# Layer 0's experts: ScalarE and VectorE take up the side work one block later, TensorE's program unchanged

## The chip, the cores and the metric

The kernel runs on one core of a Trainium2 chip. The metric is the device time of one execution in microseconds (us). Before the change it is 1907.77 us, the median of 3 runs (1901.92 to 1912.78). Engines are named as the profile does: PE is TensorE, DVE VectorE, ACT ScalarE, POOL GpSimd and SP the engine that issues the DMAs.

## The reference, cut to what matters

Two transformer layers act on x of 4 x 1024 tokens with 128 channels, each layer with 16-head attention and a mixture of experts with the best two of E gates. The stage in question begins behind the attention of layer 0:

```python
x = layernorm(x + attention0(x, Wqkv, Wout))          # causal
# experts of layer 0: E = 8, F = 256, K = 2
scores = x @ Wg.T
topk_scores, topk_idx = top_k(scores, 2)
gating = one_hot(topk_idx) weighted by softmax(topk_scores)
h = silu(x @ W1[e].T) * (x @ W2[e].T)                 # for every expert e
x = layernorm(x + sum_e gating[e] * (h @ W3[e].T))
# then layer 1: attention with rotary embedding, experts with E = 4
```

## The kernel before

Every engine has its own program, and the programs meet at semaphores only; each engine takes its instructions strictly in the written order. The stage "experts of layer 0" is `pe_end`, `act_end` and `dve_end` with `layer` 0. It treats the 4096 tokens in 8 chunks of 512 (`pe_chunk`, `act_chunk`, `dve_chunk`), and each chunk in 16 blocks n = 0 to 15, one for every 128 of the 8 x 256 hidden columns.

The main work of block n:

- TensorE, `pe_hidden` (L971): six matmuls (three partial products each for W1 and W2) put the two hidden sums into PSUM. It is issued one block ahead: in step n stands the hidden work of block n + 1 (`h_lead`).
- ScalarE: `act_s` = silu of the first sum (L1176).
- VectorE: `lin_u` = second sum times the gate row (L1375), then `hid` = `act_s` times `lin_u` (L1379).
- TensorE, `pe_product` (L1067): `hid` times W3 is summed up in `bank0`. It waits for `hid_ready`.

Beside the blocks run three other tasks, spread over the 16 steps by a table of numbers, `plan[0]`, in `pe_beside`, `act_beside` and `dve_beside`. For the chunk behind ("back"), the second layernorm and layer 1's q, k and v; for the chunk ahead ("front"), layer 0's output projection, layernorm and router. The plan gives: y_turn 1, norm2 3, x2_turn 4, q 5, k 6, v 7, o_turn 8, o_proj 9, norm 10, x_turn 11, router 12, weigh 13, g_turn 14. Most of these steps hand a result from TensorE to ScalarE or VectorE in one step, and TensorE uses their answer in the next step:

- x2_turn (4): TensorE transposes `x_out`, which VectorE normalised in step 3 (L1221). ScalarE copies it to `xt2` (L1122), which q (L1003) reads in step 5.
- q and k (5, 6): VectorE turns them by the rotary tables (`rot`, L1306 and L1307); TensorE's k and v wait for `rot_done`, since they write the same banks.
- v (7): VectorE copies `v_all` (L1312), subtracts `qk_lo` twice (L1316) and copies `os_` (L1321), for which o_turn (8) waits (`o_in`).
- o_turn (8): ScalarE copies `ot` (L1132), which o_proj (9) reads. VectorE adds and takes statistics (L1326, L1213, L1216), POOL takes the root, VectorE normalises `xs` (L1221) in step 10, and x_turn (11) waits for it.
- x_turn (11): ScalarE copies `xt` and `x_hi`, and the router (12) reads `xt`.
- router (12): VectorE finds the best two (L1229 to L1232). ScalarE's exp (L1145) and VectorE's gates (L1254 to L1275) stand in step 13, and g_turn (14) waits for them.
- g_turn (14): ScalarE copies `gate_t` (L1150), which gate row 0 of the next chunk (L980, step 15) reads.

A gate row is one matmul (L980) into the single bank `bank1`. ScalarE copies it to `gate_bc` (L1161), and the next gate row waits for that copy (`gbc_saved`). Row 0 of a chunk belongs to step 15 of the chunk before, and row e to step 2(e - 1).

How far ScalarE and VectorE are behind is set by `LATE`, one number for each layer. In step n, both do the main work of block n, and then the side work of step n - LATE. In TensorE's program `LATE` doesn't occur. At the start of chunk c the side work that is left over from chunk c - 1 comes first:

```python
m = n - LATE[layer]
if m >= 0:
    act_aside(act, st, c, m, back, front, 1 - par, layer)
elif not isinstance(c, int) or c > 0:
    act_aside(act, st, c - 1, m + SPC, None, c, par, layer)
```

Of the kernel before, what the change touches and what calls it, by code (L numbers as in the profile page):

```python
# [39 lines left out]
PAIRS_STEP = 2  # L40
SB = 3
HB = 4
LATE = (0, 2)
PAIR_HEADS = (2, 0, 3, 1)
ROWS = 2 * SLOT

# [159 lines left out]
def build_program(nc, d, out):  # L206
    with ExitStack() as ctx:
# [955 lines left out]
        def act_aside(act, st, c, n, back, front, par, layer):  # L1163

            per = SPC // n_exp[layer]
            act_beside(act, st, n, back, front, par, layer)
            e = n // per + (layer == 0)
            if n % per == per - 2 and e < n_exp[layer]:
                act_gate_rows(act, st, c, e, layer)

        def act_chunk(act, st, c, par, back, front, layer):
            for n in range(SPC):
                act.wait_ge(st.h_ready, c * SPC + n + 1)
                wait_used(act, st.hid_ready, c * SPC + n - 1)
                if layer == 0:
                    nc.scalar.activation(act_s[n % 2][:, :], hbank[n % 2], ACT.Silu).then_inc(st.s_done, 1)  # L1176
                else:
                    if n % 2 == 0:
                        wait_used(act, st.y_done, c * SPC + n - HB + 1)
                        nc.scalar.activation(hid_hi[n % HB][:, :], hbank[h_of[1][n]], ACT.Gelu, bias=be1[:, n:n + 1])  # L1180
                    nc.scalar.activation(act_s[n % 2][:, :], hbank[h_of[1][n]], ACT.Gelu,  # L1181
                                         bias=be1[:, n:n + 1]).then_inc(st.s_done, 1)
# [5 lines that stand above are left out]
            if layer == 0:  # L1188
                act.wait_ge(st.y_done, (c + 1) * SPC)
                nc.scalar.activation(y_sb[:, :], bank[0][:, :], ACT.Copy).then_inc(st.y_saved, 1)  # L1190

        def act_end(act, st, layer):
# [11 lines left out]
            act_chunk(act, st, 2 * B - 1, 1, 2 * B - 2, None, layer)  # L1204
            for n in range(SPC - LATE[layer], SPC):
                act_aside(act, st, 2 * B - 1, n, None, None, 0, layer)
# [144 lines left out]
        def dve_weigh(dve, st, c, e):  # L1351

            dve.wait_ge(st.gbc_saved, 1 + c * E1 + e + 1)
            dve.wait_ge(st.y_done, c * SPC + (e + 1) * (SPC // E1))
            if e == 0:
                wait_used(dve, st.y_turned, c)
            elif e > 1:
                dve.wait_ge(st.y_sum, 2 * c + e - 1)
            nc.vector.scalar_tensor_tensor((y_sb if e == 0 else y_tmp)[:, :], y_bank[e % 2], be2[:, e:e + 1],
                                           gate_bc[e % 2][:, :], ALU.add, ALU.mult).then_inc(st.y_used, 1)  # L1360
            if e > 0:
                dve.wait_ge(st.y_used, c * E1 + e + 1)
                nc.vector.tensor_tensor(y_sb[:, :], y_sb[:, :], y_tmp[:, :],
                                        ALU.add).then_inc(st.y_sum if e < E1 - 1 else st.y_saved, 1)

        def dve_chunk(dve, st, c, par, back, front, layer):
            per = SPC // n_exp[layer]
            for n in range(SPC):
# [12 lines left out]
                else:  # L1381
                    wait_used(dve, st.y_done, c * SPC + n - HB + 1)
                    dve.wait_ge(st.s_done, h_banks[layer] + c * SPC + n + 1)
                    if n % 2 == 1:
# [3 lines left out]
                                            ALU.subtract).then_inc(st.hid_ready, 1)  # L1388
                    if n % per == LATE[1] and (n > per or back is not None):
                        dve_weigh(dve, st, c if n > per else back, (e - 1) % E1)  # L1390
                m = n - LATE[layer]
                if m >= 0:
# [263 lines left out]
```

## Time and profile before

| | |
|---|---|
| median of 3 runs | 1907.77 us (1901.92 to 1912.78) |
| profiled execution, its own time | 1903.04 us |
| its span, first to last instruction | 1901.2 us |
| mean granted TensorE clock | 0.961 |
| busy, whole span | PE 90%, DVE 76%, ACT 63%, POOL 5% |
| experts of layer 0 | about 387 to 787 us |
| experts of layer 1 | about 1600 to 1880 us |

In the rows, a line such as "L1176 ACT ACTIVATE act_s<-hid_pair" is one instruction group with its line in the kernel, engine, operation, output and input. A timeline row has its start and its duration in front. A bracket at its end is the time for which the engine was idle before, and who ended this. Matmuls overlap in the rows: their starts show the pace, and the end of one is modelled. The share of busy time is an average over stages with different limits, so a change in one stage is read from that stage.

### The profile page before, as it was taken

What the parts mean: (1) busy time and instruction counts of PE and PEld (TensorE: products, weight loads), DVE (VectorE), ACT (ScalarE), POOL (GpSimd) and SP (SyncE); (2) the same over time, 40 slices, a digit from 0 to 9 for tenths busy, and PEclk for the clock granted to TensorE, in tenths of its full rate; (3) what the DMA queues carried; (4) which work ended last, traced back from release to release, by engine and by line L of the source; (5) the groups of instructions that cost most, each with busy time, mean ns of one, the idle gap of its engine ahead of it and who ended that gap; (6) DMA issues with size and microseconds to landing.
All of it is one profiled execution on the core that took longest, in us unless ns stands there. A gap on an engine that the chain in (4) does not pass through costs nothing.

```text
span 1901.2 us, 31713 instructions
## 1 busy us (share of the span) xinstructions
PE 1705.9 (90%) x9440; PEld 866.5 (46%) x9440; DVE 1451.9 (76%) x2661; ACT 1201.6 (63%) x1858; POOL 94.3 (5%) x123
## 2 busy tenths in 40 slices
PE   6899999799999999759999999999999986888887
PEld 3333433356565666423333333333333324656665
DVE  2788888757777777567898888889889825777776
ACT  3788888643444444206777777777777775665565
POOL 1000000001101110110000000000000000000010
PEclk9899999899999999958999999999999997998999
DMA  7431212101110011120010000000000001000000
GB/s 223 128 106 50 61 49 61 67 1 34 34 34 17 18 33 33 34 74 2 27 39 21 21 22 21 21 21 21 21 22 21 21 1 45 7 7 6 6 11 12
DMA packets 44967, 69.07 MB, mean 36 GB/s; under 512 B 16080, under 2 KB 25168, under 8 KB 44256
## 3 DMA queue, kind: packets, MB, share of 16 engines
q1 hardware_dynamic: 44896, 68.28, 12.2%
q8 instruction: 26, 0.43, 0.1%
q14 instruction: 45, 0.37, 0.1%
HBM read 42.03 MB, written 26.21 MB: 36 GB/s over the span
## 4 chain that ended last, share of the span: by engine, by line
PE 69%; DVE 13%; ACT 9%; issue 7%; DVEq 1%; DMA 1%; POOL 0%; SPq 0%; ACTq 0%; POOLq 0%
PE full_o L696 13%; PE score L683 12%; PE hid_pair L971 12%; ACT probs L745 6%; PE causal_o L458 5%; PE bank L1067 5%; PE triple L442 4%; PE max_pair L659 3%; DVE cprobs L521 2%; PE bank L980 2%; PE bank L1079 2%; PE bank L1003 2%; PE bank L897 1%; DVE negmax L783 1%; PE hid_pair L903 1%
## 5 line engine op out<-in xcount | busy, mean ns | idle before, releaser
L783 DVE TENSOR_REDUCE negmax<-max_pair 128x1 f32<-128x1024 f32 x512 | 599.6, 1217 | 71.1 <-PE max_pair L659 64.1
L745 ACT ACTIVATE probs<-score 128x512 f32<-128x512 f32 x1024 | 528.9, 604 | 151.3 <-PE score L683 151.3
L659 PE MATMUL max_pair<-k_st,q_st 64*128 64x512 f32 x1024 | 406.2, 475 | 23.4 <-DMA q_st<-q_scr 19.3
L683 PE MATMUL score<-q_st,k_st 64*128 64x512 f32 x1024 | 383.8, 452 | 33.2 <-ACT probs L745 23.9
L683 PEld LDWEIGHTS score<-q_st,k_st 64*128 64x128 f32 x1024 | 171.1, 186 | 304.4 <-ACT probs L745 283.0
L491 ACT ACTIVATE cprobs<-triple 128x1536 f32<-128x1536 f32 x192 | 268.4, 1456 | 38.7 <-PE triple L442 38.5
L696 PE MATMUL full_o<-probs,v_st 128*32 128x512 f32 x2048 | 273.2, 606 | 0.0
L659 PEld LDWEIGHTS max_pair<-k_st,q_st 64*128 64x128 f32 x1024 | 172.1, 191 | 81.4 <-DVE negmax L783 39.6
L971 PE MATMUL hid_pair<-x_hi,w_hi 128*128 128x512 f32 x384 | 181.0, 471 | 7.5 <-ACT act_s L1181 7.5
L1176 ACT ACTIVATE act_s<-hid_pair 128x512 f32<-128x512 f32 x128 | 76.4, 597 | 154.7 <-PE hid_pair L971 154.7
L521 DVE TENSOR_SCALAR cprobs<-cprobs 128x1536 f32<-128x1536 f32 (+6 forms) x272 | 162.8, 622 | 0.4 <-ACT cprobs L491 0.4
L458 PE MATMUL causal_o<-cprobs,v_st 128*32 128x512 f32 (+3 forms) x1536 | 154.7, 499 | 8.4 <-DVE o_sb L546 7.0
L971 PE MATMUL hid_pair<-x_lo,w_hi 128*128 128x512 f32 x384 | 153.0, 398 | 0.0
L971 PE MATMUL hid_pair<-x_hi,w_lo 128*128 128x512 f32 x384 | 152.0, 396 | 0.0
L442 PE MATMUL triple<-q_st,k_st 64*128 64x512 f32 (+3 forms) x768 | 143.9, 400 | 7.7 <-ACT cprobs L491 5.0
L1375 DVE TENSOR_TENSOR lin_u<-hid_pair,gate_bc 128x512 f32<-128x512 f32 x128 | 88.2, 689 | 71.9 <-PE hid_pair L971 65.8
L1067 PE MATMUL bank<-hid,w 128*128 128x512 f32 x256 | 131.4, 594 | 1.0 <-DVE hid L1379 0.7
L442 PEld LDWEIGHTS triple<-q_st,k_st 64*128 64x128 f32 x768 | 73.5, 187 | 115.4 <-issue 64.8
L1387 DVE TENSOR_TENSOR hid_lo<-act_s,hid_hi 128x512 fp32r<-128x512 f32 x128 | 86.8, 689 | 31.8 <-ACT act_s L1181 23.3
L520 DVE SCALAR_TENSOR_TENSOR cprobs<-cprobs,bound 128x512 f32<-128x512 f32 (+4 forms) x176 | 94.7, 538 | 16.0 <-ACT cprobs L491 10.6
L1181 ACT ACTIVATE act_s<-hid_pair,be 128x512 f32<-128x512 f32 x128 | 87.3, 685 | 27.1 <-DVE hid_lo L1387 14.9
L1379 DVE TENSOR_TENSOR hid<-act_s,lin_u 128x512 f32<-128x512 f32 x128 | 90.6, 708 | 11.1 <-ACT act_s L1176 6.9
(144 smaller groups left out, 1752.5 us busy)
## 6 DMA issues: line engine op xcount, KB each, us to landing
k_st<-k_scr SPq DMA_DIRECT2D x64, 128.0 KB, 2.9
q_st<-q_scr SPq DMA_DIRECT2D x128, 64.0 KB, 2.4
q_st<-q_scr SPq DMA_DIRECT2D x16, 512.0 KB
k_st<-k_scr SPq DMA_DIRECT2D x64, 104.0 KB
q_scr<-qk_hi SPq DMA_DIRECT2D x24, 256.0 KB, 2.9
k_scr<-qk_hi SPq DMA_DIRECT2D x24, 256.0 KB, 3.1
q_scr<-qk_lo SPq DMA_DIRECT2D x16, 256.0 KB, 2.9
k_scr<-qk_lo SPq DMA_DIRECT2D x16, 256.0 KB, 3.2
```

The source lines that it names most:

```text
L442: last = nc.tensor.matmul(triple[n % 2][:, bk, off:off + w], k_st[p][rows, j, kt * P:(kt + 1) * P], q_st[p][rows, q0:q0 + w], start=True, ...
L458: last = nc.tensor.matmul(causal_o[SLOT * j:SLOT * (j + 1), c0:c0 + w], v_st[p][:, kt, j, :], cprobs[at % CP][:, bk, off:off + w], start=( ...
L491: nc.scalar.activation(cprobs[n % CP][:, :, :], triple[n % 2][:, :, :], ACT.Exp, scale=SCALE).then_inc(L.exp_done, 1)
L520: nc.vector.scalar_tensor_tensor(edge, edge, float(np.exp(-CLIP)), limit, ALU.max, ALU.min)
L521: ins = nc.vector.tensor_scalar(plain, plain, float(np.exp(-CLIP)), float(np.exp(CLIP)), ALU.max, ALU.min)
L659: ins = nc.tensor.matmul(ring[slot][:, half, :], q_st[p][rows, qt * P:(qt + 1) * P], k_st[p][rows, j, half * CH:(half + 1) * CH], start=Tr ...
L683: nc.tensor.matmul(sbank[L.score_bank(e)][:, :], k_st[p][rows, j, kt * P:(kt + 1) * P], q_st[p][rows, q0:q0 + w], start=True, stop=True, t ...
L696: last = nc.tensor.matmul(full_o[SLOT * j:SLOT * (j + 1), :], v_st[p][:, kt, j, :], probs[s % NP][:, j, :], start=(kt == 0), stop=last_ste ...
L745: nc.scalar.activation(probs[s % NP][:, j, :], sbank[L.score_bank(e)][:, :], ACT.Exp, scale=SCALE).then_inc(L.exp_done, 1)
L783: nc.vector.tensor_reduce(negmax[:, qt // TPC, j, qt % TPC:qt % TPC + 1], ring[slot][:, :, :].rearrange("p a n -> p (a n)"), AXX, ALU.max, ...
L971: last = nc.tensor.matmul(hbank[2 * k + h_of[layer][n]], w[:, slice_of(n)], x[:, :], start=(a == 0), stop=(a == 2))
L1067: nc.tensor.matmul(bank[0][:, :], w3[:, n, :], hid[n % 2][:, :], start=(n == 0), stop=(n == SPC - 1)).then_inc(st.y_done, 1)
```

## The change

One number changes: `LATE` for layer 0 goes from 0 to 1.

```diff
 SB = 3
 HB = 4
-LATE = (0, 2)
+LATE = (1, 2)
 PAIR_HEADS = (2, 0, 3, 1)
```

TensorE's program is the same instruction for instruction, with the same waits. In the programs of ScalarE and VectorE the side work of step n now stands behind the main work of block n + 1. The wait values are the same. The loops before the first chunk and behind the last one do side work alone and are as they were.

VectorE in the loop over the chunks, blocks 7 and 8 (`hid1`, then `hid0`), before:

```order
L1377 REGISTER_ALU
L1379 TENSOR_TENSOR hid1<-act_s1,lin_u1 128x512
L1312 REGISTER_ALU
L1312 COPY v_all<-bank2 128x512
L1316 TENSOR_TENSOR qk_lo0<-rot0,qk_hi0 128x512
L1316 TENSOR_TENSOR qk_lo1<-rot2,qk_hi1 128x512
L1321 ISA
L1321 COPY os_<-o_tm 128x512
L1372 REGISTER_ALU
L1375 TENSOR_TENSOR lin_u0<-hid_pair1,gate_bc0 128x512
L1377 REGISTER_ALU
L1379 TENSOR_TENSOR hid0<-act_s0,lin_u0 128x512
```

The same place now:

```order
L1379 TENSOR_TENSOR hid1<-act_s1,lin_u1 128x512
L1306 TENSOR_TENSOR rot2<-bank2,rope_a 128x512
L1307 TENSOR_TENSOR rot3<-bank3,rope_b 128x512
L1372 REGISTER_ALU
L1375 TENSOR_TENSOR lin_u0<-hid_pair1,gate_bc0 128x512
L1377 REGISTER_ALU
L1379 TENSOR_TENSOR hid0<-act_s0,lin_u0 128x512
L1312 REGISTER_ALU
L1312 COPY v_all<-bank2 128x512
L1316 TENSOR_TENSOR qk_lo0<-rot0,qk_hi0 128x512
L1316 TENSOR_TENSOR qk_lo1<-rot2,qk_hi1 128x512
L1321 COPY os_<-o_tm 128x512
```

The work on v and `os_` has moved from behind block 7 to behind block 8, and the rotation of k to behind block 7.

ScalarE at the border between two chunks (`act_s1` is block 15, `act_s0` block 0 of the next chunk), before:

```order
L1150 ACTIVATE gate_t<-bank3 16x512
L1173 REGISTER_ALU
L1176 ACTIVATE act_s1<-hid_pair0 128x512
L1155 ISA
L956 ISA
L1161 ACTIVATE gate_bc0<-bank1 128x512
L1190 ACTIVATE y_sb<-bank0 128x512
L1173 REGISTER_ALU
L956 REGISTER_ALU
L1176 ACTIVATE act_s0<-hid_pair0 128x512
```

The same place now:

```order
L1176 ACTIVATE act_s1<-hid_pair0 128x512
L1150 ACTIVATE gate_t<-bank3 16x512
L1189 ISA
L1190 ACTIVATE y_sb<-bank0 128x512
L1173 REGISTER_ALU
L956 REGISTER_ALU
L1176 ACTIVATE act_s0<-hid_pair0 128x512
L1155 ISA
L956 REGISTER_ALU
L1161 ACTIVATE gate_bc0<-bank1 128x512
```

The copy of gate row 0 (`gate_bc0`) has moved behind the copy of the chunk's sum (`y_sb`) and behind the silu of the next chunk's block 0.

## Rows read from the trace of the kernel before

**Rows 1.** Windows: busy time of each engine in the stage, clock, DMA.

```profile
387.00:787.00 400.00, 390.77 (x1451) 241.96 (x1449) 279.78 (x669) 164.96 (x270) 35.55 (x42) 1.00 0.09 28
```

**Rows 2.** Waits of PE in 387 to 787 us: total, times, longest.

```profile
PE bank L1052 <- DVE g_halves L1275: 6.6, 7, 1.0
...
PE bank L1067 <- DVE hid L1379: 0.7, 1, 0.7
```

**Rows 3.** Timeline, PE, one chunk: products of blocks 8, 9, 10, 12, 13; o_proj.

```profile
514.42 1.02 PE L1067 MATMUL bank<-hid,w 128*128 128x512 f32 x2
515.29 1.05 PE L1023 MATMUL bank<-w_o,ot 128*128 128x128 f32 x8
517.56 1.02 PE L1067 MATMUL bank<-hid,w 128*128 128x512 f32 x2
520.43 1.02 PE L1067 MATMUL bank<-hid,w 128*128 128x512 f32 x2
...
526.99 1.02 PE L1067 MATMUL bank<-hid,w 128*128 128x512 f32 x2
529.24 1.02 PE L1067 MATMUL bank<-hid,w 128*128 128x512 f32 x2
```

**Rows 4.** Timeline, block 9 on ACT and DVE.

```profile
514.62 0.60 ACT L1176 ACTIVATE act_s<-hid_pair 128x512 f32<-128x512 f32 x1 [0.92 <-PE hid_pair L971]
515.42 0.69 DVE L1379 TENSOR_TENSOR hid<-act_s,lin_u 128x512 f32<-128x512 f32 x1
```

**Rows 5.** Timeline, ACT at the border of two chunks.

```profile
485.76 0.60 ACT L1190 ACTIVATE y_sb<-bank 128x512 f32<-128x512 f32 x1 [1.76 <-PE bank L1067]
...
486.73 0.61 ACT L1161 ACTIVATE gate_bc<-bank 128x512 f32<-128x512 f32 x1
```

**Rows 6.** Timeline, DVE: rotation, work on v, statistics, `xs`.

```profile
802.54 0.69 DVE L1306 TENSOR_TENSOR rot<-bank,rope_a 128x512 f32<-128x512 f32 x1 [2.14 <-PE bank L1003]
803.15 0.68 DVE L1307 TENSOR_TENSOR rot<-bank,rope_b 128x512 f32<-128x512 f32 x1
...
509.65 0.69 DVE L1312 COPY v_all<-bank 128x512 f32 x1 [0.46 <-PE bank L1009]
511.45 0.42 DVE L1321 COPY os_<-o_tm 128x512 f32 x1
...
516.56 0.69 DVE L1326 TENSOR_TENSOR res<-x_tm,bank 128x512 f32<-128x512 f32 x1 [0.45 <-PE bank L1023]
518.30 0.38 DVE L1216 BATCH_NORM_AGGREGATE mv<-st 128x2 f32<-128x6 f32 x4 [0.15 <-DVE st L1213]
520.26 1.11 DVE L1221 TENSOR_SCALAR xs<-res,mv,rstd 128x128 f32<-128x128 f32 x4 [0.24 <-POOL rstd L1427]
```

**Rows 7.** Timeline, all engines: from the router to the gates' transpose.

```profile
525.18 0.18 DVE L1229 COPY sc<-bank 128x32 f32<-128x32 f32 x1
526.92 0.17 DVE L1232 TENSOR_TENSOR lead<-mx 128x4 f32<-128x4 f32 x1
527.80 1.28 ACT L1145 ACT_TABLE_LOAD   x1
529.10 0.20 ACT L1145 ACTIVATE p<-lead 128x4 f32<-128x4 f32 x1
529.33 0.17 DVE L1254 TENSOR_SCALAR p<-p 128x4 f32<-128x4 f32 x1 [0.65 <-ACT p L1145]
530.90 0.19 DVE L1275 TENSOR_TENSOR g_halves<-gts,g_halves 128x32 fp32r<-128x32 f32 x1
531.15 0.60 PE L1052 MATMUL bank<-ident,g_halves 128*16 128x128 f32 x4 [0.90 <-DVE g_halves L1275]
```

**Rows 8.** Timeline, PE, experts of layer 1: where the clock fell.

```profile
1713.92 1.11 PE L897 MATMUL bank<-ident,os_ 128*128 128x128 f32 x4 [2.60 <-DVE os_ L1321]
```

**Rows 9.** Windows, layer 1's experts: first and last of three clock falls; PEclk third last.

```profile
1715.00:1720.00 5.00, 5.00 (x14) 3.78 (x14) 1.62 (x3) 1.88 (x3) 0.00 (x0) 0.50 0.00 2
...
1795.00:1800.00 5.00, 4.83 (x17) 3.51 (x18) 1.78 (x5) 1.88 (x3) 0.00 (x0) 0.66 0.00 0
```

## The prediction

> **What bounds the kernel now.** I read the windows of the stage first, then PE's waits, then the timeline of one chunk of the loop, because the change touches nothing outside the experts of layer 0. The reader is to see in [rows 1] that TensorE is busy 390.8 of 400 us there at a granted clock of 1.00, while VectorE has 280 and ScalarE 165. TensorE sets the time of this stage, and the other two have air. The waits view [rows 2] shows where TensorE stands still today: the largest entry is 6.6 us in 7 times, for the gates. In all its idle time is 400 - 390.8 = 9.2 us. Because the modelled end of a matmul lies behind the moment at which the next could start, I add some 0.17 us for each of three or four waits in a chunk, and count 1.7 us of waiting per chunk, 13 us in the stage.
>
> So the stage is well covered, and the question is what covers it. The timeline [rows 3] gives TensorE's beat. I set a clock to 0 where the product of block n - 1 starts; the hidden work of block n has then just been issued. The product lasts to 0.87 (514.42 to 515.29). Then TensorE comes to the side matmuls of step n, and behind them, strictly in order, stand a gate row, the six matmuls of hidden block n + 1 and the product of n. A step without side matmuls lasts 2.25 us (526.99 to 529.24), with a gate row 2.87 (517.56 to 520.43).
>
> Before the change, the answer to the side matmuls of step n is made while TensorE does hidden n + 1 and product n, some 2.25 us. This is the cover. With one block of delay the answer is made only behind silu, `lin_u` and `hid` of block n + 1, which themselves wait for hidden n + 1. TensorE, though, asks for the answer in step n + 1 as before, 0.87 us behind that point. The cover shrinks to the length of one product.
>
> **What is removed, added and moved.** No instruction with work is added or removed; the side instructions of 8 chunks move behind one more block. In TensorE's, POOL's and SP's programs nothing moves. SP's stores of q and k are issued later, but wait for VectorE's halves only, and a chunk gets longer, so I cost them at nothing; the same for POOL, whose 1.6 us of root stands in a term below. The durations stay as they are, so everything is in the waits. On ScalarE silu begins at 0.20 and ends at 0.80; `hid` ends at 1.69 (515.42 + 0.69 - 514.42) [rows 4]. Instructions in a row on ScalarE start 0.485 apart (the third of three 0.97 behind the first, 485.76 to 486.73) [rows 5], so a copy behind silu runs from 0.69 to 1.29. On VectorE the next one starts some 0.08 before the end of the last (803.15 against 802.54 + 0.69) [rows 6], so side work begins at 1.61. From an end to the waiting matmul it takes 0.06 (530.90 + 0.19 to 531.15) [rows 7]. TensorE is there at 0.87. Each new wait:
>
> - ScalarE's copies, four in a chunk: `xt2` for q, `ot` for o_proj, `xt` for the router, `gate_t` for gate row 0. 1.29 + 0.06 - 0.87 = 0.48 each, 1.92 together.
> - `x_out` (step 3) for x2_turn (4): 1.61 + 1.11 (the same operation on `xs`, [rows 6]) + 0.06 - 0.87 = 1.91.
> - Rotation of q for k (6), of k for v (7): it lasts 802.54 to 803.83, 1.29 us [rows 6]. 1.61 + 1.29 + 0.06 - 0.87 = 2.09, twice, 4.18.
> - `v_all`, two `qk_lo` and `os_` for o_turn (8): 509.65 to 511.87, 2.22 us [rows 6]. 1.61 + 2.22 + 0.06 - 0.87 = 3.02. POOL's sum and ScalarE's `qk_hi` are done before, since k's rotation ends a whole step earlier.
> - `xs` for x_turn (11). The statistics of step 9 begin at 1.61 behind block 10. From their start to the start of `xs` it takes 3.70 (516.56 to 520.26), and `xs` takes 1.11: ready at 6.48 with the handover. TensorE is there at 2.87 + 0.87 = 3.74. Wait 2.74. VectorE's block 11 fits in while POOL works.
> - Gates for g_turn (14). The best two are found in 1.91 us (525.18 to 527.09) [rows 7], now behind block 13, so to 3.52, which is 1.27 on the clock of block 14. `lin_u` and `hid` of 14 then end near 2.68. Exp is not what is late: silu to 0.80, the table load of 1.28, exp 0.22, ready at 2.30. From L1254 to the end of L1275 it takes 1.76, so to 4.44, and 4.44 + 0.06 - 0.87 = 3.63.
> - Gate row 1 of the next chunk, at the border: it waits until row 0 is copied. The product of block 15 ends at 1.02 [rows 3], `y_sb` follows at 1.06, silu of block 0 at 1.55, the copy from 2.03 to 2.64 [rows 5]. 2.64 + 0.06 - 0.87 = 1.83. Before, this copy was done ahead of `y_sb`.
>
> Sum of a chunk with both neighbours: 1.92 + 1.91 + 4.18 + 3.02 + 2.74 + 3.63 + 1.83 = 19.2 us, less the 1.7 of today: 17.5. There are six such chunks: 105. The first chunk has no chunk behind: `os_` alone ahead of o_turn (1.61 + 0.42 + 0.06 - 0.87 = 1.22), three ScalarE copies 1.44, 2.74 and 3.63, less 1.2 of today: 7.8. The last has no chunk ahead: 1.83 + 1.91 + 0.48 + 4.18 = 8.4. Together 121 us.
>
> A rule that speaks here: the Trainium skill, ScalarE: Activation LUTs, section What ACT_TABLE_LOAD costs, gives 1283 ns for a load and a further 1380 ns of drain per switch. The trace has the 1.28, but no drain: load at 527.80, exp at 529.10, 0.02 behind its end [rows 7]. With the page's drain exp would be ready at 3.68, the gates would be 1.0 us later, and seven chunks would add 7 us; by the rows nothing is added, and I go by the rows.
>
> **The clock.** The stage runs at full clock today. What waits do to it, the trace shows in layer 1's experts: at 1713.92 TensorE had stood idle for 2.60 us, after shorter gaps, and the clock fell there [rows 8]; the next 5 us ran wholly at 0.50, the lower level of 1.2 GHz; of three such falls in the stage the last shows 0.66, which is 3.4 us at half rate [rows 9]. A fall of 3.4 to 5 us loses 1.7 to 2.5 us of matmul work, say 2.0. After the change each full chunk has three waits longer than that 2.60 (3.02, 2.74, 3.63) and three of about 2. In layer 1 a wait of that kind brought a fall in only three of eight chunks. Bounds: no fall, 0; three in each of seven chunks at 2.5, 53 us. I take 10 falls, 20 us, because the waits here are longer and more, though TensorE works through between them.
>
> Time: 1903.0 (the profiled execution, of which 1901.2 is span) + 121 + 20 = 2044. The median of the runs lies 4.7 above that execution, so 2044 to 2049; I say 2046, 7.2% above 1907.77.
>
> **Rivals.**
> - No clock loss: 1903 + 121 = 2024. For it: TensorE would still be busy some three quarters of the time, and most waits like that of [rows 8] in layer 1 left the clock at full. Against: three long waits in every chunk. The Trainium skill, TensorE: Matmul & The Clock Gate, section What's actually happening, has the clock fall with idleness and come back with work; the trace agrees, 0.50 behind the idle 2.60 us.
> - Clock falls with nearly every long wait, or the half rate lasts and feeds the next wait: 1903 + 121 + 50, 2074 and above.
> - Only ScalarE's handovers cost, because VectorE, 30% free in [rows 1], gets its side work in somehow: (1.92 + 1.83) x 7 = 26, 1929. Against: VectorE's order is fixed, and nothing lets the side work pass `hid`, which waits for hidden n + 1.
> - Not slower: with the main work first, `hid` and silu never stand behind side work, and TensorE's products and hidden matmuls get their inputs earlier. The best this can give back is all of TensorE's idle time, 9.2 us: 1894. It decides if the side results have a block of slack in TensorE's program. Against: [rows 2] shows TensorE waiting for a side result (the gates) already without the delay, and only 0.7 us of the 9.2 goes to a product that waits for `hid`.
>
> **How the numbers follow.** Waits as worked, with some clock loss (2030 to 2065): 56%. No clock loss, 2024: 20%. Large clock loss, 2070 and up: 13%. ScalarE's handovers alone or a like part of the sum, 1925 to 2000: 8%. Not slower: 3%, shared by faster and the same. Below the no-loss case each term could be 10% too large, which gives 2012; above, the upper bound of the clock gives 2077. The range is 2008 to 2080. About 0.5% (10 us) is what a measurement of this kernel can tell from no change: slower by more than that 0.97, within 0.015, faster 0.015.
>
> **What would show it.** In the changed profile: the stage 520 to 545 us long in place of 400, a chunk near 69 to 72 us where it is 51 now; new entries in PE's waits for `rot`, `os_`, `xs`, `x_out`, `g_halves`, `xt2`, `ot`, `xt`, `gate_t` and `gate_bc` with the sizes above less some 0.2; ScalarE's and VectorE's busy time the same; all other stages the same; windows with a clock below 1.00 in the stage. Wrong is the prediction if PE's waits for `rot` are near zero, if a chunk stays under 60 us, or if TensorE's busy time grows by more than 30 us, which would be the clock.

## The result, and the profile after

The changed kernel takes 2069.95 us (median of 4, 2068.65 to 2076.68); the kernel before, on the same chip, 1904.85. The ratio is 1.0868, 95% interval 1.0823 to 1.0914: slower by 165 us. I had said 2046 with a range of 2008 to 2080. The way and the range hold, but the increase over the profiled 1903.0 was forecast as 141 and is 165.6.

The whole increase lies in the experts of layer 0. The rows for the 128 silus of the stage (count, duration, first and last start) show it, first before, then after:

```profile
L1176 ACT ACTIVATE act_s<-hid_pair x128: 596/597/601, 389.3 to 784.5; 128x512 f32<-128x512 f32 x128
```

```profile
L1176 ACT ACTIVATE act_s<-hid_pair x128: 592/597/598, 387.3 to 948.3; 128x512 f32<-128x512 f32 x128
```

From first to last silu it is 395.2 us before and 561.0 after, +165.8. I use this length below for every run. The windows of exactly these stretches, before and then after (PE, PEld, DVE, ACT, POOL busy, PEclk, DMA):

```profile
389.30:784.50 395.20, 386.70 (x1442) 240.30 (x1443) 278.40 (x667) 163.07 (x268) 35.55 (x42) 1.00 0.09 28
```

```profile
387.30:948.30 561.00, 446.98 (x1442) 262.49 (x1443) 275.54 (x667) 153.71 (x268) 35.41 (x42) 0.90 0.06 20
```

VectorE and ScalarE do the same work; ScalarE's 154 in place of 163 comes from more instructions that stand right behind another and overlap in the rows, with the same counts. TensorE stands idle for 114 us where it was 8.5, and it is busy for 60 us more with the same 1442 matmul records: that is the clock, 0.90 in the mean where it was 1.00 (compare [rows 1]). PE's waits in the stage name each handover. They answer to [rows 2]:

```profile
PE bank L1052 <- DVE g_halves L1275: 24.0, 7, 3.4
PE bank L897 <- DVE os_ L1321: 18.4, 7, 2.9
PE bank L897 <- DVE xs L1221: 18.3, 7, 2.6
PE bank L897 <- DVE x_out L1221: 15.9, 8, 5.0
PE bank L1003 <- DVE rot L1307: 13.7, 7, 2.0
PE bank L1009 <- DVE rot L1307: 13.4, 7, 1.9
PE bank L980 <- ACT gate_bc L1161: 11.7, 7, 1.7
PE bank L1003 <- ACT xt L1122: 2.9, 8, 0.7
```

(The 5.0 of `x_out` belongs to the side work behind the last chunk, which is there in both kernels. Of ScalarE's four copies only `xt2`, the last row, makes TensorE wait in every chunk with a chunk behind; `ot`, `xt` and `gate_t` have one wait of 0.3 each.) On the clock of a block, the larger waits come out as worked. The timeline of PE in one chunk, from x_turn on (without the hidden matmuls):

```profile
570.10 1.02 PE L1067 MATMUL bank<-hid,w 128*128 128x512 f32 x2
573.74 0.66 PE L897 MATMUL bank<-ident,xs 128*128 128x128 f32 x4 [2.62 <-DVE xs L1221]
...
583.19 1.02 PE L1067 MATMUL bank<-hid,w 128*128 128x512 f32 x2
587.63 0.60 PE L1052 MATMUL bank<-ident,g_halves 128*16 128x128 f32 x4 [3.43 <-DVE g_halves L1275]
...
593.93 1.02 PE L1067 MATMUL bank<-hid,w 128*128 128x512 f32 x2
596.66 0.49 PE L980 MATMUL bank<-gate_t,expert_row 16*128 16x512 f32 x1 [1.71 <-ACT gate_bc L1161]
...
606.66 1.12 PE L1067 MATMUL bank<-hid,w 128*128 128x512 f32 x2
609.17 0.66 PE L897 MATMUL bank<-ident,x_out 128*128 128x128 f32 x4 [1.38 <-DVE x_out L1221]
...
616.21 1.02 PE L1067 MATMUL bank<-hid,w 128*128 128x512 f32 x2
619.18 3.48 PE L1003 MATMUL bank<-xt,w_qkv 128*128 128x512 f32 x4 [1.95 <-DVE rot L1307]
...
629.99 1.02 PE L1067 MATMUL bank<-hid,w 128*128 128x512 f32 x2
633.90 1.11 PE L897 MATMUL bank<-ident,os_ 128*128 128x128 f32 x4 [2.90 <-DVE os_ L1321]
```

Start of the waiting matmul less start of the product less 0.87 gives, worked against measured: `xs` 2.74, 2.77; gates 3.63, 3.57; gate row 1.83, 1.86; `x_out` 1.91, 1.64; rotation of q 2.09, 2.10; `os_` 3.02, 3.04. The rows also show what I had mis-sized. The four matmuls of k last 3.48 us at 619 where they took 1.88, and the transposes at 633.90 last 1.11 where they took 0.66. Windows of 5 us around the waits for the gates and for `os_`:

```profile
585.00:590.00 5.00, 2.37 (x10) 1.92 (x11) 2.31 (x10) 1.77 (x3) 0.00 (x0) 0.88 0.00 0
590.00:595.00 5.00, 4.95 (x12) 2.04 (x10) 1.38 (x2) 1.07 (x3) 0.00 (x0) 0.78 0.01 3
595.00:600.00 5.00, 3.34 (x14) 2.31 (x15) 2.57 (x4) 2.69 (x5) 0.00 (x0) 1.00 0.00 0
...
630.00:635.00 5.00, 2.10 (x8) 0.95 (x6) 3.53 (x6) 1.11 (x2) 0.00 (x0) 0.82 0.02 5
635.00:640.00 5.00, 5.00 (x10) 2.94 (x10) 1.26 (x2) 1.37 (x3) 0.00 (x0) 0.50 0.95 309
```

Summed over the stage in windows of 0.5 us, as (1 - PEclk) / 0.5 of their length, TensorE ran for 116 us at half rate, in 28 falls, four in a full chunk. Set beside PE's waits, a fall begins in the wait or within 1.5 us behind its end: at all seven waits for the gates, all seven for `xs`, the six for `os_` in the chunks of the loop (these falls last 6.8 us, the others 3.4), all seven for the rotation of q, and one of seven for `gate_bc`. None begins at the seven for the rotation of k or the seven for `x_out`.

### The profile page after: what moved, and what is told of

The parts are those of the page before. It is cut to its first block, busy times and chain, and to the rows that moved or that the text cites. A ratio compares the mean times of both kernels' runs of the same rounds, so it can differ in the third digit from the quotient of the medians.

```text
span 2066.8 us, 31719 instructions
## 1 busy us (share of the span) xinstructions
PE 1766.8 (85%) x9440; PEld 890.0 (43%) x9440; DVE 1449.6 (70%) x2661; ACT 1192.4 (58%) x1858; POOL 94.6 (5%) x123
## 4 chain that ended last, share of the span: by engine, by line
PE 63%; DVE 17%; ACT 8%; issue 7%; SPq 1%; DVEq 1%; DMA 1%; POOL 1%; ACTq 0%; POOLq 0%
PE full_o L696 12%; PE hid_pair L971 12%; PE score L683 11%; ACT probs L745 6%; PE causal_o L458 5%; PE triple L442 4%; PE bank L1067 4%; PE max_pair L659 3%; PE bank L1003 2%; DVE cprobs L521 2%; PE bank L980 2%; DVE lin_u L1375 2%; PE bank L897 1%; PE bank L1079 1%; PE max_pair L670 1%
## 5 line engine op out<-in xcount | busy, mean ns | idle before, releaser
L971 PE MATMUL hid_pair<-x_hi,w_hi 128*128 128x512 f32 x384 | 187.4, 488 | 7.2 <-ACT act_s L1181 7.2
L971 PE MATMUL hid_pair<-x_lo,w_hi 128*128 128x512 f32 x384 | 160.3, 417 | 0.0
L971 PE MATMUL hid_pair<-x_hi,w_lo 128*128 128x512 f32 x384 | 159.8, 416 | 0.0
L1067 PE MATMUL bank<-hid,w 128*128 128x512 f32 x256 | 147.4, 660 | 1.1 <-DVE hid L1379 0.7
L971 PEld LDWEIGHTS hid_pair<-x_hi,w_hi 128*128 128x128 f32 x384 | 75.5, 197 | 48.9 <-issue 30.3
```

The lines of the kernel that those rows point to most:

```text
L971: last = nc.tensor.matmul(hbank[2 * k + h_of[layer][n]], w[:, slice_of(n)], x[:, :], start=(a == 0), stop=(a == 2))
L1067: nc.tensor.matmul(bank[0][:, :], w3[:, n, :], hid[n % 2][:, :], start=(n == 0), stop=(n == SPC - 1)).then_inc(st.y_done, 1)
```

## The experiments

My theory: 121 us are the handovers that lost their cover, and the other 44 are matmuls at half rate. Rivals: the 44 are more waiting; one side of the change carries most of it; a wait that is taken away comes back at another place.

**filler.** TensorE gets more work. Ahead of seven of the waits, matmuls are added whose result is overwritten by the next hidden work:

```diff
+FILL = {4: 6, 6: 7, 7: 7, 8: 11, 11: 10, 14: 13}
+FILL_GATE = 6
+        def pe_fill(pe, st, c, par, n, many):
+            ...
+            for k in range(many):
+                nc.tensor.matmul(hbank[h_of[0][(n + 1) % SPC]], w_hi[0][:, slice_of(n)], x_hi[par][:, :], start=True,
+                                 stop=True)
```

> The changed kernel with matmuls added whose results are thrown away: in each full chunk TensorE does 6 of them ahead of x2_turn, 7 ahead of k and of v, 11 ahead of o_turn, 10 ahead of x_turn, 13 ahead of g_turn and 6 ahead of gate row 1, each about 0.23 us, so that they fill most of a wait and end before it does. They write a bank that the hidden work of the next block overwrites. Theory (waits of 121 us, and on top some 44 us because the waits let TensorE's clock fall to half rate): TensorE has more work, the waits end when they did, the clock stays near 1.00 in the stage, and the time falls from 2070 to about 2026 (1905 + 121), range 2015 to 2040. Rival (the 44 us are more waiting, not clock: a wait that I sized too small or a copy slowed by TensorE's traffic): the added matmuls change nothing or cost, 2070 or above. If the clock falls in spite of the added work: 2070 and up, with a clock near 0.90.

Measured: 2029.54 us (2024.28 to 2032.71) against 1908.45 for the kernel before, ratio 1.0631 (1.0587 to 1.0674), so 121 us slower. The windows from first to last silu:

```profile
387.00:905.10 518.10, 493.51 (x1855) 314.49 (x1856) 275.24 (x667) 154.07 (x267) 35.45 (x42) 1.00 0.07 22
```

The clock stays at 1.00 and the stage is 122.9 us longer than before (518.1 - 395.2); the waits alone had been worked out as 121. With 413 more matmul records the kernel is some 40 us faster than without. That settles the split: 43 us of the 166 (561.0 - 518.1) are the clock. At full clock all four of ScalarE's copies show in PE's waits, seven times each, 2.2 to 2.5 us in sum; in the changed kernel three of them were hidden behind matmuls at half rate.

**fill_long.** As filler, with `FILL = {8: 11, 11: 10, 14: 13}` and `FILL_GATE = 0`.

> The changed kernel with the thrown-away matmuls only ahead of the three long waits (o_turn, x_turn, g_turn); the waits for x_out, both rotations and the border stay empty. In the changed kernel the clock was at half rate for 116 us in 29 falls, 43 us lost; with all waits filled in none, and nothing lost. Theory (long waits cost the clock, those of about 2 us seldom): nearly all falls go, 2030 to 2038. Rival (the two waits for the rotation, two steps in a row, are enough for a fall, as one at 619 us in the changed kernel suggests): one fall per chunk stays at about 3.5 us of half rate, 0.37 us lost for each, so 9 us or a little more, 2038 to 2048. Rival (falls only move to another wait): 2055 and above.

Measured: 2048.16 us against 1907.47, ratio 1.0742 (1.0719 to 1.0766), 141 us slower. That is at the upper end of the second case, and the mechanism is its own but wider: waits of 1.4 to 2 us cost the clock too. Of the ten falls inside the stage six begin at the rotation of q, three at `x_out` and one at `gate_bc`, and with 48 us at half rate they come to twice the 3.5 us per chunk that was expected. One chunk, with a fall behind each of these two waits:

```profile
748.77 0.66 PE L899 MATMUL bank<-ident,x_out 128*128 128x128 f32 x4 [1.40 <-DVE x_out L1241]
...
756.99 1.02 PE L1069 MATMUL bank<-hid,w 128*128 128x512 f32 x2
759.96 3.62 PE L1005 MATMUL bank<-xt,w_qkv 128*128 128x512 f32 x4 [1.95 <-DVE rot L1327]
```

The stage is 539.4 us long (392.7 to 932.1), 144.2 more than before, with 54 us at half rate, 6 of these at its start.

**act_late, dve_late.** Each takes one half of the change, by a number of its own for ScalarE:

```diff
+LATE_ACT = (1, 2)    # act_late, with LATE = (0, 2); dve_late: LATE_ACT = (0, 2), with LATE = (1, 2)
-                m = n - LATE[layer]
+                m = n - LATE_ACT[layer]
```

> The kernel before with ScalarE alone one block late (LATE 1 in act_chunk, 0 in dve_chunk). Theory, from the same clock of a block: four copies 0.48 us each, gate row 1 at the border 1.83, o_turn 1.64 (the second qk_hi comes behind silu of block 8 and VectorE stands waiting for it), the gates 3.3 in place of 1.05, because exp is behind silu of block 14 and VectorE stands idle for it: 8.8 per chunk less 1.7 of today, in all 49 us and 5 to 15 us of clock, 1955 to 1970. Rival (only ScalarE's own copies cost, VectorE's waits for ScalarE are covered): 20 to 26 us, 1925 to 1931. Rival (ScalarE's lateness carries most of the change): above 2000.

Measured: 1973.72 us against 1908.45, ratio 1.0342 (1.0305 to 1.0379), 65 us, a little above the range. PE's waits, the four largest of the stage:

```profile
PE bank L1053 <- DVE g_halves L1276: 17.7, 7, 2.6
PE bank L981 <- ACT gate_bc L1162: 11.7, 7, 1.7
PE bank L898 <- DVE os_ L1322: 8.5, 6, 1.4
...
PE bank L1068 <- DVE hid L1380: 3.8, 9, 0.7
```

Two of the three largest are waits for VectorE, which isn't late in this kernel: it stands behind `qk_hi` and exp, as expected. The sizes are less good: the gates' wait is 2.5 in the mean, 2.7 with the 0.17 that the waits view leaves out, where 3.3 was worked, and products wait for `hid` (3.1 us between first and last silu, the row counts a little further), which was not worked at all. The two nearly cancel in the sum of 49. The first rival, 20 to 26 us, falls, and so does the second, above 2000.

> The changed kernel with ScalarE back to no delay (LATE 0 in act_chunk, 1 in dve_chunk). Theory: the copies and the border wait go, x2_turn 1.91, k and v 2.09 each, o_turn 3.02 and x_turn 2.74 stay, and the gates' wait grows from 3.6 to about 5.0, because exp must wait for the best two before silu of block 14 and the second table load stands ahead of silu, so that VectorE's hid of block 14 is late: 16.9 per chunk less 1.7, in all 105 us and 25 to 45 us of clock, 2035 to 2055. Rival (the two halves of the change add up without a bond between them: 165 less what ScalarE alone costs): with act_late at 1963, 2011 to 2015. The gates' wait in the profile tells them apart: 5.0 against 3.6 and below.

Measured: 2072.28 us against 1908.45, ratio 1.0853 (1.0814 to 1.0892), 164 us. The gates' wait is as worked:

```profile
PE bank L1053 <- DVE g_halves L1276: 34.4, 7, 4.9
```

But the time misses both forecasts upward. The mean clock of the stage is 0.87, and 145 us ran at half rate, where the changed kernel has 116. So VectorE's half alone costs as much as the whole change: fewer handovers wait, but the longest wait is longer and the clock is down longer. The halves don't add up (65 + 164 against 165).

**os_early.** In the changed kernel, the copy of `os_` goes behind the rotation of q:

```diff
-                if n == pl.o_turn - 1:
+                if n == (pl.q if layer == 0 else pl.o_turn - 1):
```

> The changed kernel with one VectorE copy moved in layer 0: os_ is copied behind the rotation of q (side work of step 5) and no longer behind v_all and qk_lo (step 7). Theory (each wait is worth its own length, plus the clock that it costs): the wait ahead of o_turn, 3.02 us worked and 3.04 measured, goes to zero in six chunks, and 1.2 us in the first: 19 us of waiting, and 0 to 15 us of clock, so 2036 to 2051. Rival (the time is set by VectorE's whole row of late work, and another wait takes this one's place, since v_all and qk_lo now stand against o_proj and block 9): under 6 us gained, 2064 to 2070.

Measured: 2052.09 us against 1908.45, ratio 1.0754 (1.0715 to 1.0794); 144 us slower than before instead of 165, so 21 us won. The wait for `os_` is gone from PE's waits, and the half-rate time is 93 us. The theory's gain is there and the rival's isn't. In the stage, 23.5 us shorter, 14 of these are idle time of TensorE (100 in place of 114) and 9 its busy time, which is the clock. The idle time falls by less than the 19 worked because small waits for ScalarE's copies are back: for `ot` 2.2 us in 7 times where it was 0.3 in one, for `xt` 1.7 and for `gate_t` 1.5 where they were 0.3 each.

**gate0_early.** In the changed kernel, gate row 0 of the next chunk is copied ahead of `y_sb` again:

```diff
-                elif not isinstance(c, int) or c > 0:
+                elif layer == 1 and (not isinstance(c, int) or c > 0):
                     act_aside(act, st, c - 1, m + SPC, None, c, par, layer)
             if layer == 0:
+                act_aside(act, st, c, SPC - 1, back, front, 1 - par, layer)
                 act.wait_ge(st.y_done, (c + 1) * SPC)
```

> The changed kernel with one ScalarE copy moved: gate row 0 of the next chunk is copied right ahead of y_sb again, as before the change, and all other side work stays one block late. Theory: seven waits of 1.83 us go, 12.8 us, with up to 5 us of clock, so 2052 to 2058. Rival (product of block 0 and its gate row then wait for hid or y_sb instead): 2065 to 2070.

Measured: 2065.07 us against 1907.47, ratio 1.0840 (1.0816 to 1.0864). That is 158 us slower, 7.5 won where 12 to 18 were expected. The time is the rival's (2065 to 2070), but its mechanism isn't there: the wait for `gate_bc` is gone from PE's waits, and no wait for `hid` or `y_sb` has come in the stage. The stage is 552.6 us long (390.9 to 943.5), 8.4 shorter. TensorE's idle time falls by 12.3 us (101.7 in place of 114.0), close to the 12.8 of the theory, and its busy time rises by 3.9. The half-rate time is 121 us in place of 116, and the 5 more lie at the very start of the stage; behind it the clock gave nothing back for the seven waits that went. Why the start of the stage ran at half rate in this profiled run was not tried.

**plan.** The kernel before with o_turn in step 3 and the front's later steps one earlier, the gates' transpose staying at 14:

```diff
-        for pl, steps in ((plan[0], (1, 3, 4, 5, 6, 7, 8, 9, 10, 11, None, 12, 13, 14)),
+        for pl, steps in ((plan[0], (1, 3, 4, 5, 6, 7, 3, 8, 9, 10, None, 11, 12, 14)),
...
+                        if k == 0 and layer == 0 and front is not None:
+                            pe.wait_ge(st.ot_ready, front + 1)
...
+                    if layer == 0 and back is not None:
+                        pe.wait_ge(st.stats2, back + 1)
```

> The kernel before (no delay in layer 0) with another plan: o_turn goes from step 8 to step 3, o_proj, norm, x_turn, router and weigh one step earlier each (8, 9, 10, 11, 12), g_turn stays at 14, so that the gates have two steps. Two waits on semaphores are added on TensorE for the bank that o_turn now shares. Theory (a handover costs only what its cover lacks): the gates' wait of 1.05 us and that for os_ of 0.43 go, nothing new comes, 10 us gained, 1895 against 1905. Rival (o_proj at 8 now waits for v_all, or q for ot, and takes it back): within 3 us of before. Rival (o_proj ahead of x_out's follow-ups loads VectorE in steps 7 and 8, and x_turn waits longer): 5 us or more slower.

Measured: 1903.52 us (12 runs) against 1907.47 (17 runs), ratio 0.9981 (0.9968 to 0.9994): 4 us faster than before (by the interval 1 to 6), and less than the 10 expected. By the time alone the first rival, within 3 us, is not excluded; by the waits it is, since no wait for `v_all` or `ot` has come. In the six chunks of the loop TensorE's waits for the gates (5.7 us) and for `os_` (1.6 us) are gone, and a wait of a product for `hid` has come:

```profile
PE bank L1071 <- DVE hid L1383: 2.2, 6, 0.4
```

A full chunk takes 50.3 us from one `y_sb` to the next in place of 51.2, 5 us in six. In the profiled run the stage also began at half rate: from 387 us on 11 us of it, where the kernel before had 2.5. Why, and whether the other runs did so, was not tried.

All runs together (the waits are those worked out on the clock of a block, not measured; the rest is the increase less them; the time at half rate is that between first and last silu):

| run | stage, first to last silu | increase | waits, worked | left | at half rate |
|---|---|---|---|---|---|
| after | 561.0 | 165.8 | 121 | 45 | 116 |
| dve_late | 562.1 | 166.9 | 105 | 62 | 145 |
| gate0_early | 552.6 | 157.4 | 108 | 49 | 121 |
| os_early | 537.5 | 142.3 | 102 | 40 | 93 |
| fill_long | 539.4 | 144.2 | 121 | 23 | 54 |
| act_late | 463.2 | 68.0 | 49 | 19 | 47 |
| filler | 518.1 | 122.9 | 121 | 2 | 0 |

What is left over is 0.39 to 0.44 of the time at half rate in every run but filler, which has no half rate and 2 us left. It would be 0.5 if TensorE had only useful, uncovered matmuls in that time.

## Why the prediction was right, and where it was off

- What bounds the stage (TensorE, with a cover of one block for each answer) was right: the side work cost nothing until its cover went, though no instruction was added.
- The waits step by step were right in the main. Five of the six read above agree within 0.06 us and `x_out` within 0.27, and their sum of 121 is what filler measured at a full clock (121 us in the medians, 122.9 in the stage). In the changed kernel itself the idle time grew by 105.5 us only (114.0 less 8.5) and the busy time by 60.3, since some of the waits, those of 0.48 for ScalarE's copies above all, lie behind matmuls at half rate.
- That POOL, SP and the other stages stay as they were was right: the stage's 165.8 is the 165 of the whole.
- The rule of a drain behind a table load, from the Trainium skill, ScalarE: Activation LUTs, section What ACT_TABLE_LOAD costs, is not borne out here: the load stands at 584.00 for 1.28 us and exp begins at 585.29, and the wait for the gates was 3.57 where the rows gave 3.63 and the page's drain would, as an estimate, have given 4.6.
- The clock term was mis-sized. I took "10 falls, 20 us"; there were 28, four in a chunk, and 43 us. The step that failed is "In layer 1 a wait of that kind brought a fall in only three of eight chunks", which misreads the trace of before. TensorE waits for `os_` seven times there, and only two of these waits last 2.60 us, at 1713.92 ([rows 8]) and at 1795.17. Both brought a fall. The third fall, from about 1754.5, stands behind a wait of 1.53. The case for the rival without clock loss, "most waits like that of [rows 8] in layer 1 left the clock at full", rests on the same misreading:

```profile
1753.90 0.66 PE L897 MATMUL bank<-ident,os_ 128*128 128x128 f32 x4 [1.53 <-DVE os_ L1321]
...
1795.17 0.65 PE L897 MATMUL bank<-ident,os_ 128*128 128x128 f32 x4 [2.60 <-DVE os_ L1321]
```

- So the rows of before already spoke for a fall at every wait of 2.6 us and over, and for some at shorter ones. The changed kernel has 20 such waits (six for `os_`, seven each for `xs` and the gates), each with its fall, and eight falls at waits of 1.7 to 2 us. Why the rotation of q always brought one and that of k never is open.
- The first fall in layer 1 was also read too short: in windows of 0.5 us it lasts 6.8 us, and not up to 5. Yet the loss of 2.0 us for a fall was too large: 43 us over 28 falls is 1.5, because a matmul at half rate partly runs while TensorE would have waited anyway.
- By two of the signs named beforehand the waits were right: the waits for `rot` are there, and a chunk is not under 60 us. By the third, "if TensorE's busy time grows by more than 30 us, which would be the clock", the prediction was wrong, in its clock term: the busy time grew by 60. The stage (561 us) and a full chunk (75.1) also lie above the 520 to 545 and 69 to 72 given, and waits for `ot`, `xt` and `gate_t` were to be seen and hardly are.
- That the time still fell into the range owes something to luck. The upper end counted 21 falls at 2.5 us, 53 us; there were more falls at a smaller loss each, and the two errors work against each other.
- The likeliest case reached only to 2065. The time lies between it and "large clock loss, 2070 and up", to which I gave 13%; with a fall at every long wait and 43 us lost, the mechanism is nearer to that rival, which counted 50.
- The rivals "ScalarE's handovers alone" and "not slower" fell with the waits view. "No clock loss" fell with the clock of 0.90. act_late showed besides that ScalarE's delay reaches further than its own copies, through VectorE.

## What to carry to other kernels

When in-order engines hand results to and fro, a step of the plan is worth its cover: count what the asking engine does between its request and its need, and put one side's work later only if the plan of the other moves too (the last is a conclusion, no run here moved both). Work the waits out on the clock of one block; then add a clock term for every stage in which TensorE begins to wait several times in a row, and measure it by filling the waits with matmuls that are thrown away. If the time falls and the granted clock rises, as in filler, the loss was the clock.

## What the runs showed of the hardware that was not expected

- More work made the kernel faster: 413 more matmul records in the stage, 2029.5 in place of 2070 us.
- All the falls of the clock inside the stage lasted 3.4 or 6.8 us in the windows of 0.5 us, in all six kernels that had them; only those that were under way at its start show less.
- Shortening waits changed where the clock fell and not only how often: gate0_early has 12 us less idle time and, its start left out, the same 116 us at half rate as the changed kernel, with four falls at the waits for `x_out`, where the changed kernel has none.
- In fill_long, with the three long waits filled, the clock still fell at waits of 1.4 to 2.0 us.
